# First layer of an audio tower: k's masked blocks by eight DMAs from one copy, rounded conv and down, weights prepared between the slots

## The reference, cut to what matters

```python
h = _L0_tok_ref(x, ...)            # y = einsum(pairs of frames, conv_w) + conv_b + mean of the pair; layer norm
h = h + _L0_attn_ref(_layernorm(h), qkv_proj, qkv_bias, out_proj, out_bias)   # 16 heads of 16, softmax over 64
h = h + _L0_ffn_ref(_layernorm(h), w_gate, w_up, w_down)
#   fp4_linear(x, w) = fp4_quant_dequant(x) @ fp4_quant_dequant(w).T
#   h = silu(fp4_linear(x, w_gate)) * fp4_linear(x, w_up); return fp4_linear(h, w_down)
h = h + _L1_attn_ref(_layernorm(h), ...)
h = h + _L1_ffn_ref(h, ...)
```

## Time and profile before

| | |
|---|---|
| median of 3 runs | 4660.76 us (4659.73 to 4663.47) |
| the profiled execution | 4667.47 us, span 4665.6 us |
| mean granted TensorE clock | 0.985 |
| busy, share of the span | PE 95%, PEld 85%, DVE 71%, ACT 57%, POOL 42% |
| first layer | the first conv starts at 74.98 us, the loads of the second layer begin at 1749.72 |

### The profile page before, as it was taken

The page is one execution under the profiler, slowest core; times in us unless marked ns, Lnnn a source line. Parts: engine busy times, 40 slices in busy tenths (PEclk is TensorE's granted clock), DMA queues, the critical chain, the costliest instruction groups (busy, mean ns, idle before and its releaser), DMA issues.

```text
span 4665.6 us, 119233 instructions
## 1 busy us (share of the span) xinstructions
PE 4432.7 (95%) x43016; PEld 3952.5 (85%) x43016; DVE 3333.5 (71%) x6915; ACT 2640.0 (57%) x5596; POOL 1959.1 (42%) x2582
## 2 busy tenths in 40 slices
PE   3999999999999985999999999999999999999997
PEld 2888888888888864899999999999999999998986
DVE  4888888888888863566666666666666666666665
ACT  2666666666666643455555555555555555555553
POOL 1455555555555531334334334334334334334333
PEclk9999999999999997999999999999999999999998
DMA  2000000000000001000000000000000000000000
GB/s 84 20 24 20 24 24 24 22 22 24 24 24 21 23 15 39 8 8 8 15 9 8 15 9 8 15 9 8 15 9 8 15 9 8 15 9 8 15 5 11
DMA packets 64945, 79.30 MB, mean 17 GB/s; under 512 B 8758, under 2 KB 51126, under 8 KB 64438
## 3 DMA queue, kind: packets, MB, share of 16 engines
q1 hardware_dynamic: 64566, 74.07, 5.4%
HBM read 49.40 MB, written 24.64 MB: 16 GB/s over the span
## 4 chain that ended last, share of the span: by engine, by line
PE 56%; DVE 2%; issue 1%; ACT 1%; POOL 1%; DMA 0%; ACTq 0%; DVEq 0%; SPq 0%; POOLq 0%
PE bA L938 11%; PE bA L939 9%; PE bA L940 9%; PE bS L1223 4%; PE bO L1245 3%; PE bA L1307 3%; PE bB L938 2%; PE bB L1208 2%; PE bB L1209 2%; PE bB L940 2%; PE bB L939 2%; PE bA L1308 2%; PE bT L1261 2%; PE bO L1254 1%; PE bO L1249 1%
## 5 line engine op out<-in xcount | busy, mean ns | idle before, releaser
L1638 POOL TENSOR_TENSOR sqs_lo<-sq,sqs_hi 128x768 fp32r<-128x768 f32 x256 | 477.9, 1867 | 676.7 <-ACT sqs_hi L1358 673.1
L1449 DVE TENSOR_TENSOR qk_lo<-bA,qk_hi 128x384 fp32r<-128x384 f32 x512 | 284.5, 556 | 538.6 <-ACT qk_hi L1358 538.5
L1377 ACT ACTIVATE phi<-bB 128x768 f32<-128x768 f32 x256 | 207.4, 810 | 665.1 <-PE bB L1209 665.1
L1596 POOL TENSOR_TENSOR yT_lo<-tanh_y,yT_hi 128x384 fp32r<-128x384 f32 x256 | 259.4, 1014 | 556.8 <-ACT yT_hi L1358 556.8
L1358 ACT ACTIVATE qk_hi<-bA 128x384 fp32r<-128x384 f32 x512 | 251.6, 491 | 203.7 <-PE bA L940 203.5
L1459 DVE TENSOR_TENSOR aT<-bS,mask 128x1024 f32<-128x1024 f32 x256 | 311.0, 1215 | 2.0 <-PE bS L1228 1.3
L1367 ACT ACTIVATE sq<-bA 128x384 f32<-128x384 f32 x512 | 250.3, 489 | 62.0 <-DVE qk_lo L1449 61.8
L518 PE MATMUL bank<-down_sb,hqT 128*128 128x256 f32 x1128 | 278.7, 389 | 1.0 <-ACT hqT L600 1.0
L616 ACT ACTIVATE kblk<-gu,kb_masked,rowmask 128x128 f32<-128x128 f32 x752 | 271.3, 463 | 8.1 <-PE gu L542 8.1
L518 PEld LDWEIGHTS bank<-down_sb,hqT 128*128 128x128 f32 x1128 | 204.3, 190 | 52.8 <-issue 32.6
L938 PE MATMUL bA<-fc_lo,yT_hi 128*128 128x256 f32 x768 | 230.6, 300 | 12.9 <-ACT pre L1407 6.2
(11 more groups left out here) (245 smaller groups left out, 15104.2 us busy)
## 6 DMA issues: line engine op xcount, KB each, us to landing
xT<-in_x SPq DMA_DIRECT2D x94, 256.0 KB, 2.6
h_scratch<-h SPq DMA_DIRECT2D x188, 64.0 KB, 1.9
hx<-h_scratch SPq DMA_DIRECT2D x32, 256.0 KB, 2.7
out<-res SPq DMA_DIRECT2D x32, 256.0 KB, 2.2
hx<-h_scratch SPq DMA_DIRECT2D x64, 64.0 KB, 2.5
out<-res SPq DMA_DIRECT2D x64, 60.0 KB, 1.8
q<-in_fc_q SPq DMA_DIRECT2D x2, 1024.0 KB, 6.4
wq_sb<-in_wq SPq DMA_DIRECT2D x1, 1024.0 KB, 5.0
```

The costliest lines, as they stand in the source:

```text
L1449: dve.tensor_tensor(dst, src, hi.bitcast(fp32), ALU.subtract).then_inc(S[done], 1)
L1638: pool.tensor_tensor(sqs[1][:], sq[:], sqs[0][:].bitcast(fp32), ALU.subtract).then_inc(S["sq_lo"], 1)
```

## The change

- **k.** `qk_product` computes k first, into `gu[:, 1]`, and signals it apart from q, which stays in `gu[:, 0]`. `k_copy` on ScalarE makes one copy, `kT`, in two instructions and moves ahead of the two magnitudes. SP's new stage `k_blocks`, last in its slot, spreads it: eight DMAs of 16 partitions each copy one head's rows into their place in `kblk`, whose other rows are zero from the start. `scores` waits for all eight.
- **Rounding.** xT is split by ScalarE (`x_copy`) and GpSimd (`x_low`); hqT by ScalarE (`hq_copy`, as before, into float32r) and VectorE (`hq_low`, new); `conv` and `down` become `product3`.
- **Weights.** The first block is gone. conv's weights and x are loaded first, and the work on gate, up and down is put ahead of slots 0 to 4 (`weights(t)` on every engine): scales and rounding on VectorE, both multiplications on GpSimd, magnitudes on ScalarE, transposes in groups in the banks `pt` and `sc`. The loads of the second layer's weights are issued ahead of slot 5.

```diff
-        down_sb = sb("down_sb", [128, len(F0C), DM])
+        down_w0 = tuple(sb(f"down_{p}", [128, len(F0C), DM], fp32r) for p in ("hi", "lo"))
...
+        conv_w0 = tuple(sb(f"conv_{p}", [128, 2 * KC, DM], fp32r) for p in ("hi", "lo"))
...
+        xTs = sb("xT_hi", [128, 2 * KC, 128], fp32r), sb("xT_lo", [128, 2 * KC, 128], fp32r)
...
         qT = sb("qT", [128, KC, 128])
-        kblk = sb("kblk", [128, KC, 2, 4, 64])
+        kT = sb("kT", [128, KC, 128])
+        kblk = sb("kblk", [128, KC, 4, 128])
...
-        hqT = sb("hqT", [128, len(F0C), 128])
+        hqT = tuple(sb(f"hqT_{p}", [128, len(F0C), 128], fp32r) for p in ("hi", "lo"))
...
-        QK, YS, H1S, ST1, HH, SHIFT, ATT = KC + 4 * KC, 3, 3, 2, 4, 2, 2
...
+        QK, YS, H1S, ST1, HH, SHIFT, ATT = 2 * KC, 3, 3, 2, 4, 2, 2
+        KB = 8
...
                 def load(t, par):
-                    wait(sp, "conv_done", t - 1)
+                    wait(sp, "x_low", t - 1)
...
+                def k_blocks(t):
+                    wait_step(sp, "qk_copied", t, QK, KC)
+                    for j in range(4):
+                        for r in range(2):
+                            p = slice(64 * r + D0 * j, 64 * r + D0 * (j + 1))
+                            sp.dma_start(kblk[p, :, j, :], kT[p, :, :]).then_inc(S["kblk_ready"], 16)
+
                 def slot(t, par):
                     if exists(t, -1):
                         load(t + 1, 1 - par)
                     if exists(t, 4):
                         store(t - 4, par)
...
+                    if exists(t, 0):
+                        k_blocks(t)
...
                 def v_product(t):
-                    bank_free(pe, t, [("hh_step", t - 4, HH, HH)], [("vblk_ready", t - 2, 4, 4)])
+                    bank_free(pe, t, [("qk_copied", t - 1, QK, KC)], [("hh_step", t - 4, HH, HH), ("vblk_ready", t - 2, 4, 4)])
...
                 def conv(t, par):
                     bank_free(pe, t, [("h2_ready", t - 5, 1, 1)], [("h1_step", t - 3, H1S, 1), ("y_step", t - 1, YS, 1)])
-                    pe.wait_ge(S[f"x_loaded{par}"], t * 8 + (16 - 8 * par))
+                    wait(pe, "x_low", t + 1)
                     for c in range(2 * KC):
-                        last = pe.matmul(cv[:, 0:DM], xT[par][:, c, :], conv_sb[:, c, :], start=c == 0,
-                                         stop=c == 2 * KC - 1)
+                        last = product3(pe, cv[:, 0:DM], [x[:, c, :] for x in xTs], [w[:, c, :] for w in conv_w0],
+                                        c == 0, c == 2 * KC - 1)
...
                     wait(pe, "qk_copied", t, QK)
+                    wait(pe, "kblk_ready", t, 16 * KB)
...
-                                                 qT[p, c, 64 * n:64 * n + 64], kblk[p, c, n, :, :], start=True, stop=True)
+                                                 qT[p, c, 64 * n:64 * n + 64], kblk[p, c, :, 64 * n:64 * n + 64], start=True, stop=True)
...
-                    wait(pe, "hqT_copied", t - 3, 2)
+                    wait(pe, "hqT_split", t - 3, 2)
                     for f, (o, w) in enumerate(F0C):
-                        last = pe.matmul(cv[:, 0:DM], hqT[0:w, f, :], down_sb[0:w, f, :], start=f == 0,
-                                         stop=f == len(F0C) - 1)
+                        last = product3(pe, cv[:, 0:DM], [x[0:w, f, :] for x in hqT], [x[0:w, f, :] for x in down_w0],
+                                        f == 0, f == len(F0C) - 1)
...
-                    bank_free(pe, t, [("hh_step", t - 3, HH, 3)], [("qk_copied", t - 1, QK, QK)])
+                    if isinstance(t, int) and t == 0:
+                        pe.wait_ge(wqkv, 16 * 3)
+                    bank_free(pe, t, [("hh_step", t - 3, HH, HH)], [("qk_copied", t - 1, QK, QK), ("vblk_ready", t - 1, 4, 4)])
                     wait(pe, "ln1T_copied", t + 1)
-                    for w, o in ((q_sb, 0), (k_sb, 256)):
+                    for b, w in ((1, k_sb), (0, q_sb)):
                         for m in range(KC):
                             for c in range(KC):
-                                last = pe.matmul(gu[:, 0, o + 128 * m:o + 128 * (m + 1)], w[:, c, 128 * m:128 * (m + 1)],
+                                last = pe.matmul(gu[:, b, 128 * m:128 * (m + 1)], w[:, c, 128 * m:128 * (m + 1)],
                                                  ln1T[:, c, :], start=c == 0, stop=c == KC - 1)
-                    last.then_inc(S["qk_done"], 1)
+                        last.then_inc(S["qk_done"], 1)
...
                 def q_copy(t):
+                    wait(act, "qk_done", t + 1, 2)
                     for m in range(KC):
                         act.activation(qT[:, m, :], gu[:, 0, 128 * m:128 * (m + 1)], ACT.Identity,
                                        bias=qb_col[:, m:m + 1]).then_inc(S["qk_copied"], 1)
 
                 def k_copy(t):
-                    wait(act, "qk_done", t + 1)
+                    wait_step(act, "qk_done", t, 2, 1)
                     wait(act, "scores_done", t)
                     for c in range(KC):
-                        src = gu[:, 0, 256 + 128 * c:256 + 128 * (c + 1)].rearrange("p (n k) -> p n k", n=2)
-                        for j in range(4):
-                            act.activation(kblk[:, c, :, j, :], src, ACT.Identity, bias=kb_masked[:, c, j:j + 1],
-                                           scale=rowmask[:, j:j + 1]).then_inc(S["qk_copied"], 1)
+                        act.activation(kT[:, c, :], gu[:, 1, 128 * c:128 * (c + 1)], ACT.Identity,
+                                       bias=kb_col[:, c:c + 1]).then_inc(S["qk_copied"], 1)
...
+                def x_copy(t, par):
+                    act.wait_ge(S[f"x_loaded{par}"], t * 8 + (16 - 8 * par))
+                    wait(act, "conv_done", t)
+                    copy(xTs[0][:], xT[par][:], "x_high")
...
+                    if exists(t, -1):
+                        x_copy(t + 1, 1 - par)
...
+                def hq_low(t):
+                    wait(dve, "hqT_copied", t - 3, 2)
+                    dve.tensor_tensor(hqT[1][:, 0:5, :],
+                                      pt[:].rearrange("p a b -> p (a b)")[:, 0:640].rearrange("p (f t) -> p f t", t=128),
+                                      hqT[0][:, 0:5, :].bitcast(fp32), ALU.subtract).then_inc(S["hqT_split"], 1)
+                    dve.tensor_tensor(hqT[1][0:64, 5, :], pt[0:64, 1, 128:256], hqT[0][0:64, 5, :].bitcast(fp32),
+                                      ALU.subtract).then_inc(S["hqT_split"], 1)
...
                         glu_up(t - 3, 0)
+                    if exists(t, 4):
+                        hq_low(t)
                     if exists(t, 2):
...
+                def x_low(t, par):
+                    wait(pool, "x_high", t + 1)
+                    pool.tensor_tensor(xTs[1][:], xT[par][:], xTs[0][:].bitcast(fp32), ALU.subtract)\
+                        .then_inc(S["x_low"], 1)
...
                         rsqrt(t, 0)
+                    if exists(t, -1):
+                        x_low(t + 1, 1 - par)
...
+                def weight_scaled(n):
+                    pool.wait_ge(W[n]["scales"], SCALE_OPS)
+                    fp4_scaled(pool, wflat[n], wflat[n], wsmall_t[n], 2, 128, width[n]).then_inc(W[n]["scaled"], 1)
+
+                def weight_values(n):
+                    pool.wait_ge(W[n]["round"], ROUND2_OPS)
+                    fp4_scaled(pool, wflat[n], wflat[n], wsmall_t[n], 1, 128, width[n]).then_inc(W[n]["ready"], 1)
...
+                    if t == 1:
+                        weight_scaled("gate")
+                        weight_scaled("up")
+                        pool.wait_ge(wfold, 5 + KC)
+                    if t == 2:
+                        weight_values("gate")
+                        weight_values("up")
+                        weight_scaled("down")
+                    if t == 3:
+                        weight_values("down")
```

More of the change, by code:

```diff
@@ new lines, in layer0 @@
+        wconv, wsmall, wqkv, wout = sem("wconv"), sem("wsmall"), sem("wqkv"), sem("wout")
+        wconst, vones, wfold, vbias = sem("wconst"), sem("vones"), sem("wfold"), sem("vbias")
+        wconv_hi, wconv_lo = sem("wconv_hi"), sem("wconv_lo")
+        wpad, wtrans, whigh, wlow = sem("wpad"), sem("wtrans"), sem("whigh"), sem("wlow")
+        W = {n: {k: sem(f"{n}_{k}") for k in ("loaded", "scales", "scaled", "abs", "round", "ready")}
+             for n in ("gate", "up", "down")}
+        wraw = {"gate": sb("graw", [128, GROUPS, DM]), "up": sb("uraw", [128, GROUPS, DM]), "down": sb("draw", [128, KC, F0])}
@@ L388, in wait_stored, with slots @@
                 eng.wait_ge(S[f"{name}{par}"], t * 16 + (32 - 16 * par))
-        def slots(eng, slot):
+        def slots(eng, slot, weights):
             first = 6
@@ L590, in slot, with weight_rows @@
                         pv_product(t, 1 - par)
-                pe.wait_ge(wfold, 6 + 2 * KC)
-                pe.wait_ge(wcopied, len(JOBS))
-                pe.wait_ge(wlow, 2)
-                slots(pe, slot)
```

(21 more changed lines are left out.)

323 lines of the change are left out of this document (175 added, 148 removed).

## The result

The changed kernel takes **5255.98 us** (median of 4 runs, 5249.84 to 5262.75), the kernel before 4661.43: a ratio of 1.1276 [1.1256, 1.1295]. The profiled execution spans 5249.3 us, 583.7 more than before. The direction and the mechanism are those of the prediction; the time lies 136 us over the upper end of its range.

The account below looks back on a forecast made before the run. TensorE bounds the kernel at 17.18 us a slot, VectorE close behind. 89 slots x (20.95 - 17.18) = +336, start -25: 4667.5 + 311 - 6.7 = 4972 us; range 4780 to 5120.

Parts of the forecast that it names:

- The bound and the chain: First layer: TensorE sets the pace; afterwards scores wait for h2_add, two stores, eight SP issues and landing, 19.5 us a slot.
- low-clock slot: A steady-loop slot in which TensorE falls to 1.2 GHz after idling: 2.4 us later, 21.9 us in all.
- Landing: Time for a k block's copy within SBUF to arrive after its issue: 1.8 us taken, bounds 1.8 and 2.5.
- I take a distance of 0.45: SP's k blocks: 0.45 us between issues, seven distances for eight DMAs; bounds 0.35 and 0.58.
- the fall in six slots of ten: TensorE's clock drops after 3.2 us idle before the scores in 0.6 of slots, 2.4 us each; mean slot 20.95.
- this state: Rival: each slot's DMA wait brings the low clock back, so every slot lasts 21.9 us; total 5056, chance 0.16.
- the sum: Profiled execution 4667.5 plus 311 us (slots +336, start -25), before taking off 6.7 to reach the median.
- The start: Before the steady loop: first conv starts 63 us sooner, quantisations between slots 0 to 4 cost 38; -25, between -45 and 0.
- TensorE's work: Rounded down 2.14 and conv 1.43 us, together 1.24 less; TensorE needs 15.9 us a slot.
- The eight small transfers are slower than the rows say: Rival on k's DMAs: landing 2.5, issue 0.58, low clock every slot, 23.5 us a slot; total 5197, chance 0.10.
- The blocks land sooner: Rival on k's DMAs: landing 1.0 us after issue, as nothing touches HBM; total 4901, chance 0.08.
- The faster rival: Eight SP issues overlap, the chain hides behind VectorE's 16.7 us a slot; total 4593, chance 0.05.

Follow-up runs that it names:

- the kernel with fourteen fillers: The changed kernel plus fourteen matmuls of 512 columns per slot, results unread, ahead of the scores' wait for the k blocks: 5025.59 us, ratio 1.078.
- the kernel with the masked copies: Against the changed kernel: k's part as before (ScalarE's eight masked copies), down in float32 without hq_low; conv rounded, weights between slots: 4624.02 us, ratio 0.992.

## Why the prediction was wrong in size

- **The bound and the chain: right.** In the low-clock slot I put h2_add at 13.14 + 2.4 - 0.42 = 15.1 after the scores; it is at 15.17. Landing: 1.8 taken, 1.9 measured. The wait for the blocks is TensorE's only long one, as forecast.
- **The step that failed: "I take a distance of 0.45" between SP's issues.** It is 0.65, and so above the 0.58 that I had as its bound. Seven distances make 7 x 0.2 = 1.4 us. With 0.1 for the landing and smaller differences the chain at the full clock is 21.15 and not 19.5. The rows that I priced it from, a load of 1 KB and halves of a store pair, were DMAs of another shape. What costs the 0.2 wasn't found. It isn't the number of partitions, since 32 instead of 16 don't change it, and it need not be the shape: the pair of stores, which the change leaves as it was, takes 1.27 to 1.30 us in place of 1.15 to 1.18.
- **The second: "the fall in six slots of ten".** It falls in all of them. The longer idle time, 4.65 and not 3.2, isn't needed for that: with the blocks ahead of the stores the clock fell in every slot after only 2.35 us. So the share was wrong by itself, not through the first error. The rows at hand, an idle of 1.62 that kept the clock and one of 3.66 that lost it, left it open where between them the fall begins. Its price was forecast at 2.4 and is 2.7. The Trainium skill, page "TensorE: Matmul & The Clock Gate", section "HAM oscillation — how this bites in real kernels", described this state, and the trace agrees; I gave it 0.16.
- Together: 21.15 - 19.5 = 1.65 for the chain and 2.74 - 0.6 x 2.4 = 1.30 for the clock, 2.95 a slot; 23.89 - 20.95 = 2.94 was missing. Over 88 slots that is 259 of the 272 us by which the profiled execution (5251.0) lies above the sum (4667.5 + 311).
- **The start: somewhat better, and given back.** Slot 5's conv starts 33 us ahead and tile 4's scores 28.5 (133.00, before 161.50) where I had 25. I had no term for the 4 MB ahead of x, which takes 9 us back in slot 5.
- **TensorE's work: 16.4 us and not 15.9.** The three-product conv takes 1.62 us and down 2.40 up to the next transposes, in place of 1.43 and 2.14. It costs nothing here, since it lies in idle time. That TensorE was done 16.3 us after the scores, as forecast (in the kernel with fourteen fillers 16.4), is luck: the work was put 0.45 too low, and the wait of conv for h2_add that I added isn't there, conv follows the product before it without a gap.
- **The rivals.** "The eight small transfers are slower than the rows say", with 23.5 a slot, came nearest, but by its issue and not by its landing. "The blocks land sooner" fell: 16 KB within SBUF land in 1.9 us, as long as 64 KB to HBM. By the Trainium skill, page "DMA: Bandwidth & Descriptors", section "Anatomy of one DMA — SWDGE (gpsimd) path", HBM is the heaviest target, so they should have been sooner; that section describes DMAs of GpSimd and these are SP's, and the measurement decides. The faster rival had its point in an issue of 0.15 us, far from the truth.
- The range was too narrow on one side: the bound of an issue was taken from the nearest rows without any room above them, though the term counts sevenfold, and its upper end held every slot slow but only a little more for the issues.

## What to carry to other kernels

A cost that is multiplied by a count, such as the issue of a DMA, needs a bound well above its nearest row, above all where being late also lowers TensorE's clock. Ask of each DMA in a loop what stands ahead of it in its queue: moving the eight ahead of two stores gave back half of the loss, a second queue most of the rest. And a transfer that nobody reads for a slot may stand behind 4 MB; once the head of an engine's slot reads it, that is paid: 12 us in slot 5 of the kernel with the masked copies.

## What the runs showed of the hardware

- The issue distance on SP for these copies within SBUF is 0.65 us for 16 KB in 16 partitions and for 32 KB in 32, and 0.70 (3.50 for five) while ScalarE's queue issues too.
- ScalarE's DMA issues stand behind q's copies in the program, yet the first starts at 607.72, ahead of the copies at 608.43: its sequencer ran ahead of the engine. The issues took nothing from its work: from the copy of k to those of q lie 2.03 us (606.40 to 608.43), and 2.01 with all eight on SP ahead of the stores.
- TensorE's clock after a wait, where nothing else stood still in the slot for longer: kept after 0.68 and 1.28 us, lost after 2.35, 3.64 to 3.77 and 4.65, and now one, now the other after 2.11 and 2.15. The fall needn't come at once: after a wait of 3.76 in the kernel with conv and down in float32 the scores still took 1.09, and the matmuls from little over a microsecond later on were slow.
- The fall has no single price: 2.7 us a slot in the change, where the granted clock over the 8 us from the start of the scores is 0.65, and 1.5 with four DMAs, where it is 0.79.
- Low clock and late blocks hold each other: fourteen useless matmuls made the changed kernel 230 us faster.
